# Layer 1's hyperbolic half-steps enter at step 1, their second maxima are dealt over steps 0 to 6, and the formula over steps 6 to 8

## The chip, the cores and the metric

The kernel runs on one core of a Trainium2 chip. The metric is the device time of one execution in microseconds. Durations in the rows below are of one profiled execution.

## The reference

Four sequences (batches) of 1024 tokens with 128 channels pass through two layers. Each layer is attention over 16 heads of 8 channels, then a mixture of experts, both with a layer norm modulated per batch in front. In layer 1 the 16 heads are of three kinds: six ordinary, four hyperbolic, six with normalised queries and keys. The hyperbolic ones are

```
inner = q·k - tq*tk
arg = max(-curv * inner, 1 + 1e-07)
scores = 1 / (1e-06 + sqrt(1/curv) * arccosh(arg)) + causal mask
out = softmax(scores) @ v
```

## The kernel before

**Layout.** The program goes through the batches in turn. Each of its engines has its own written-out program (`tensor_program`, `scalar_program`, `vector_program`, `pool_program`, `sync_program`), and they meet at semaphores. Nothing is scheduled at run time: an engine takes its instructions in the order in which the functions emit them.

**Steps of layer 1's attention.** Heads go in units of four. Units 0, 1 and 2 are ordinary softmax and run one after another, 12 steps each, 36 steps in all. A step is one block of 128 keys against the queries of one half (`c`) of the sequence that may see it; its width is 512, 384, 256 or 128 queries. Widths within a unit are 512, 384, 256, 128, then five times 512, then 384, 256, 128. In step `p` TensorE computes the scores of step p+1 (`scores`), ScalarE takes the exponentials of step p (`std_exp`, L1011, one for each pair of heads), GpSimd cuts the diagonal blocks, and TensorE multiplies with the values (`values`, L747).

**Hyperbolic half-steps.** Unit 3 is hyperbolic. Its 12 steps are split into 24 half-steps of two heads (widths 512, 512, 384, 384, ...), and one half-step enters each ordinary step from `HYP_AT` on. Half-step k passes through: `hyp_scores` (TensorE, L717, last thing in the step in which it enters); one step later `hyp_arg` (VectorE, L1344 and L1349), `hyp_root` (ScalarE, L983 and L984), and a sum on GpSimd (L1624); two steps later `hyp_score` (ScalarE, L989, L992, L995) and `hyp_shift` (VectorE, L1357), which subtracts the row's maximum; three steps later `hyp_exp` (ScalarE, L1000) and `hyp_values` (TensorE, L772).

**Banks.** The scores of ordinary pairs and of hyperbolic half-steps share two pairs of PSUM banks in turn (`take_banks`). So `hyp_scores` in step p waits until ScalarE has taken the first exponential of step p+1, and the second pair of the scores of step p+2 waits for `hyp_arg`'s first instruction.

**Side jobs.** `side_plan` deals further work over the steps: `piece` jobs (TensorE computes a block of scores at L628, with a mask at L631 on the diagonal, and VectorE reduces it to row maxima at L1284), `maxima` jobs on VectorE, `max` jobs that turn the maxima so that they can be sent to DRAM and back, and `turn` jobs for finished outputs. TensorE does up to three side jobs between the scores of a step and the rest after its values. It has two banks for them, so each waits until VectorE has emptied the one before the last. VectorE does about half of a step's side jobs ahead of `hyp_shift` and the rest behind it.

**The maxima of the hyperbolic unit** come in two halves, (0,) for the first 512 rows and (1,) for the rest. Each half passes the same formula as a score: VectorE (L1236, L1242, L1243), ScalarE (L970, L971), VectorE (L1246), ScalarE (L973, L975 four times, L978), VectorE (L1250). Before, `hyp_max` on ScalarE and `maxima` on VectorE run that in one go, at the end of step 4 for half (1,).

Of the kernel before, what the change touches and what calls it, by code (L numbers as in the profile page):

```python
# [86 lines left out]
HYP_AT = 2  # L87
HYP_HALVES = 2 * NS

# [5 lines left out]
POSITIONS = (UNITS * NS, max(3 * NS, HYP_AT + HYP_HALVES + 3) + 1)  # L95
# [7 lines left out]
def score_jobs(l):  # L103

    steps = STD_UNITS[l] * NS
    jobs = [(False, 0, 0), (False, 0, 1)]
    for p in range(POSITIONS[l]):
        if p + 1 < steps:
            jobs += [(False, p + 1, 0), (False, p + 1, 1)]
        if l and 0 <= p - HYP_AT < HYP_HALVES:  # L110
            jobs.append((True, p - HYP_AT, (p - HYP_AT) % 2))
    return jobs
# [5 lines left out]
def output_order(l):  # L118

    outs = [(NS * u + 4 + 8 * c, u, c) for u in range(STD_UNITS[l]) for c in range(NC)]  # L120
    if l:
        outs += [(HYP_AT + 2 * (4 + 8 * c) + 3, HYP_UNIT, c) for c in range(NC)]
    return sorted(outs)
# [5 lines left out]
def side_plan(l, more):  # L129
# [18 lines left out]
    if l == 0:  # L148
        pieces(0, -1, -1)
        plan[-1].append(("max", (0, BOTH)))  # L150
        if more:
            plan[0].append(("out", (0,)))
            plan[1].append(("out", (1,)))
        for u in range(1, UNITS):
            first = NS * (u - 1)
            pieces(u, first, first + NS - 4)
            plan[first + NS - 3].append(("max", (u, BOTH)))
    else:
        pieces(HYP_UNIT, -1, -1, (0,))
        plan[1].append(("max", (HYP_UNIT, (0,))))  # L160
        pieces(HYP_UNIT, 0, 4, (1,))
        plan[6].append(("max", (HYP_UNIT, (1,))))
        pieces(1, 6, 9)
        plan[10].append(("max", (1, BOTH)))
        pieces(2, 13, 21)
        plan[22].append(("max", (2, BOTH)))
        if more:
            for c in range(NC):
                plan[23].append(("xT", (c,)))
                plan[24 + c].append(("stats0", (c,)))  # L170
                plan[26 + c].append(("norm0", (c,)))
                plan[28 + c].append(("hT", (c,)))
                plan[30 + c].append(("kp", (c,)))
        for i, (p, u, c) in enumerate(OUTS[l]):
            plan[min(p + 2, POSITIONS[l])].append(("turn", (i, u, c)))
    n = 0
    for p in sorted(plan):
        items = []
        for kind, what in plan[p]:
            on_pe = kind not in ("maxima", "stats0", "norm0")  # L180
# [58 lines left out]
def adaln_kernel(nc, ins, out):  # L239
    with ExitStack() as ctx:  # L240
# [300 lines left out]
        def tensor_program(pe, b):  # L541
# [18 lines left out]
            def attention(l):  # L560
# [229 lines left out]
                for p in range(POSITIONS[l] + 1):  # L790
# [105 lines left out]
        def scalar_program(act, b):  # L896
# [47 lines left out]
            def attention(l):  # L944
# [21 lines left out]
                def hyp_max(c):  # L966
# [4 lines left out]
                    nc.scalar.activation(z, z, ACT.Exp, scale=0.5).then_inc(hyp_s, 1)  # L971
                    act.wait_ge(hyp_mx, 2 * c + 2)
# [42 lines left out]
                if l:  # L1015
                    hyp_max(0)
                for p in range(POSITIONS[l]):
                    if p < steps:
                        std_exp(p)
                    if l:  # L1020
                        k = p - HYP_AT
                        if 0 <= k - 3 < HYP_HALVES:
                            hyp_exp(k - 3)
                        if 0 <= k - 2 < HYP_HALVES:
                            hyp_score(k - 2)
                        if 0 <= k - 1 < HYP_HALVES:
                            hyp_root(k - 1)
# [61 lines left out]
        def vector_program(dve, b):  # L1089
# [120 lines left out]
            def attention(l):  # L1210
# [6 lines left out]
                def maxima(u, chunks):  # L1217
# [21 lines left out]
                    if is_hyp(l, u):  # L1239

                        c = chunks[0]
# [3 lines left out]
                        dve.wait_ge(hyp_s, 2 * c + 1)  # L1245
                        nc.vector.tensor_tensor(z, z, x, ALU.add).then_inc(hyp_mx, 1)  # L1246
                        dve.wait_ge(hyp_s, 2 * c + 2)
                        if c:
                            dve.wait_ge(a.side, count("max", (HYP_UNIT, (0,))))
                        nc.vector.tensor_scalar(m, z, -1.0, None, ALU.mult).then_inc(a.nmp, 1)  # L1250
# [120 lines left out]
                for p in range(POSITIONS[l] + 1):  # L1371
# [3 lines left out]
                    k = p - HYP_AT  # L1375
                    if l and 0 <= k - 1 < HYP_HALVES:
                        hyp_arg(k - 1)
# [3 lines left out]
                    if l and 0 <= k - 2 < HYP_HALVES:  # L1381
                        hyp_shift(k - 2)
# [162 lines left out]
        def pool_program(pool, b):  # L1545
# [70 lines left out]
            for p in range(POSITIONS[1]):  # L1616
                if p < STD_UNITS[1] * NS:
                    cut(1, p)
                k = p - HYP_AT
                if 0 <= k - 3 < HYP_HALVES:  # L1620
                    hyp_cut(k - 3)
                if 0 <= k - 1 < HYP_HALVES:
                    pool.wait_ge(h_root, k)
                    nc.gpsimd.tensor_tensor(hyp_z(b, k - 1), hyp_z(b, k - 1), hyp_x(k - 1), ALU.add).then_inc(h_sum, 1)  # L1624
# [299 lines left out]
```

## Time and profile before

| | |
|---|---|
| runs without the profiler | 2758.28, 2766.61, 2769.98 us; median 2766.61 |
| the profiled execution | 2764.56 us, span of its instructions 2762.6 us |
| mean granted TensorE clock | 0.81 of full |
| TensorE matmul busy | 2252.7 us (82% of the span) |
| VectorE busy | 1553.4 us (56%) |
| ScalarE busy | 1380.8 us (50%) |
| GpSimd busy | 660.7 us (24%) |

"Busy" is the time in which an engine had an instruction running. A granted clock of 0.5 is 1.2 GHz and 1.0 is 2.4 GHz. The shares are means over very different stages. The change touches only layer 1's attention, which occurs four times, so the rows below come from one of these four.

### The profile page before, as it was taken

Reading aid. Unit: us, or ns where it says so; the run is one execution under the profiler, and the core shown is the slowest. Engines: PE = TensorE matmul, PEld = TensorE weight load, DVE = VectorE, ACT = ScalarE, POOL = GpSimd, SP = SyncE. Lnnn points to the kernel's source line nnn. Section 1 sums busy time; section 2 is a strip of 40 time slices with the busy share of each in tenths; the row PEclk is TensorE's granted clock in tenths of the full one; section 3 lists DMA queues with packets and bytes.
Section 4 is the critical chain, followed back from the end, with each engine's and each line's share of the span. In section 5 each row is a group of like instructions: output and inputs, shape, how many; then the busy total and the mean of one; then the engine's idle time right before and its main releaser. Section 6 shows DMA issues by size and latency. Waiting matters only on the chain. (4 is left out here: it accounts for less than half of the span.)

```text
span 2762.6 us, 30066 instructions
## 1 busy us (share of the span) xinstructions
PE 2252.7 (82%) x10649; PEld 861.1 (31%) x10649; DVE 1553.4 (56%) x3429; ACT 1380.8 (50%) x1963; POOL 660.7 (24%) x639
## 2 busy tenths in 40 slices
PE   3899867778999896777998987768799998677789
PEld 1222432224433242222443234122343324322234
DVE  2564466666555256675655526566655534666542
ACT  1145426894234532898324452489522454268932
POOL 1012202332422210333331120133242111023324
PEclk9599965568999995667999987566799999655689
DMA  5200230001500023100430012210061002300012
GB/s 140 53 19 2 73 81 31 18 1 48 142 23 19 2 77 92 33 2 1 121 89 23 2 37 79 55 33 1 12 151 43 19 1 77 77 31 18 1 43 88
DMA packets 67845, 128.31 MB, mean 46 GB/s; under 512 B 11396, under 2 KB 24836, under 8 KB 63076
## 3 DMA queue, kind: packets, MB, share of 16 engines
q1 hardware_dynamic: 67696, 126.40, 17.2%
q8 instruction: 84, 1.38, 0.2%
q14 instruction: 65, 0.53, 0.1%
HBM read 109.99 MB, written 15.20 MB: 45 GB/s over the span
## 5 line engine op out<-in xcount | busy, mean ns | idle before, releaser
L1284 DVE TENSOR_REDUCE mx<-ps 128x1 f32<-128x512 f32 (+3 forms) x1248 | 641.5, 553 | 461.1 <-PE ps L631 335.9
L1011 ACT ACTIVATE pr<-ps 128x1024 f32<-128x1024 f32 (+3 forms) x672 | 515.9, 804 | 457.6 <-PE ps L701 455.2
L628 PE MATMUL ps<-kop,qop 72*128 72x512 bf16 (+6 forms) x1248 | 455.7, 388 | 142.1 <-DVE mx L1284 103.9
L701 PE MATMUL ps<-qop,kop 75*128 75x512 bf16 (+7 forms) x1344 | 419.6, 379 | 92.3 <-DVE wb L1344 32.7
L1571 POOL TENSOR_SCALAR_AFFINE_SELECT pr<-pr 128x512 f32<-128x512 f32 x224 | 149.5, 668 | 951.6 <-ACT pr L1011 950.6
L747 PE MATMUL ps<-pr,vt 128*32 128x512 f32 (+3 forms) x2688 | 360.4, 615 | 7.2 <-POOL pr L1571 6.1
L1068 ACT ACTIVATE pr<-ps 128x512 f32<-128x512 f32 x224 | 133.8, 597 | 344.1 <-PE ps L854 280.5
L628 PEld LDWEIGHTS ps<-kop,qop 72*128 72x128 bf16 (+1 forms) x1248 | 124.6, 103 | 551.0 <-DVE mx L1284 329.4
L701 PEld LDWEIGHTS ps<-qop,kop 75*128 75x128 bf16 (+1 forms) x1344 | 125.1, 107 | 328.6 <-ACT pr L1011 127.2
L631 PE MATMUL ps<-maskqk,identb 128*128 128x128 bf16 x832 | 202.3, 251 | 0.0
L864 PE MATMUL ps<-pr,w_down 128*128 128x512 f32 x384 | 197.7, 600 | 3.1 <-POOL pr L1562 3.1
L851 PE MATMUL ps<-hT,w_gate 128*128 128x512 f32 x384 | 196.1, 592 | 0.2 <-DVE on L1509 0.2
L754 PE MATMUL ps<-pr,ones 128*32 128x512 f32 (+3 forms) x1536 | 167.3, 508 | 0.0
L1334 DVE COPY osb<-ps 128x512 f32<-128x512 f32 x64 | 44.1, 689 | 213.6 <-PE ps L754 176.0
L1562 POOL TENSOR_TENSOR pr<-on,wb 128x512 f32<-128x512 f32 x84 | 106.3, 1265 | 142.3 <-DVE on L1509 130.9
L854 PE MATMUL ps<-hT,w_up 128*128 128x512 f32 x256 | 130.7, 592 | 0.0
L1344 DVE TENSOR_SCALAR wb<-ps 128x1024 f32<-128x1024 f32 (+3 forms) x96 | 91.7, 955 | 66.2 <-PE ps L717 65.4
L717 PE MATMUL ps<-qop,kop 84*128 84x512 bf16 (+3 forms) x192 | 69.4, 457 | 66.2 <-ACT pr L1011 66.1
L1624 POOL TENSOR_TENSOR wb<-wb 128x1024 f32<-128x1024 f32 (+3 forms) x36 | 72.4, 2010 | 174.1 <-ACT wb L984 174.1
L851 PEld LDWEIGHTS ps<-hT,w_gate 128*128 128x128 f32 x384 | 72.2, 190 | 88.8 <-issue 73.2
L631 PEld LDWEIGHTS ps<-maskqk,identb 128*128 128x128 bf16 x832 | 90.1, 108 | 30.8 <-issue 24.2
L1509 DVE TENSOR_TENSOR on<-pr,ps 128x512 f32<-128x512 f32 x84 | 57.4, 683 | 64.2 <-ACT pr L1068 63.8
(298 smaller groups left out, 3001.8 us busy)
## 6 DMA issues: line engine op xcount, KB each, us to landing
wb<-gates_scratch SPq DMA_DIRECT2D x192, 256.0 KB, 3.3
kop<-kparts_scratch SPq DMA_DIRECT2D x32, 576.0 KB
qop<-qparts_scratch SPq DMA_DIRECT2D x96, 192.0 KB
on<-hmax_scratch SPq DMA_DIRECT2D x8, 1024.0 KB, 5.3
kparts_scratch<-on SPq DMA_DIRECT2D x12, 256.0 KB, 2.9
qparts_scratch<-on SPq DMA_DIRECT2D x12, 256.0 KB, 4.7
qparts_scratch<-wb SPq DMA_DIRECT2D x12, 256.0 KB, 2.9
kparts_scratch<-wb SPq DMA_DIRECT2D x12, 256.0 KB, 2.8
```

Of the source, the lines that this page charges most:

```text
L628: mm = pe.matmul(o, qop[0:k, slot(l, u), j, qb * P:(qb + 1) * P], kop[0:k, slot(l, u), j, k0:k0 + wd], start=True, stop=not diag)
L631: mm = pe.matmul(o[:, wd - P:wd], identb[:], maskqk[:], start=False, stop=True)
L701: mm = pe.matmul(o, kop[0:k, slot(l, u), 2 * pair + j, kb * P:(kb + 1) * P], qop[0:k, slot(l, u), 2 * pair + j, q0:q0 + wd], start=True, s ...
L747: mm = pe.matmul(ps[32 * j:32 * j + 32, 4, o0:o0 + wd], vt[:, kb, 32 * h:32 * h + 32], pr[:, g % 3, j, o0:o0 + wd], start=kb == 0, stop=la ...
L754: mm = pe.matmul(ps[32 * j:32 * j + 32, 5, o0:o0 + wd], ones32[:], pr[:, g % 3, j, o0:o0 + wd], start=kb == 0, stop=last, tile_position=(0 ...
L851: mm = pe.matmul(ps[:, f.gate_banks[i % R], :], wt, h, start=True, stop=True)
L854: mm = pe.matmul(ps[:, 4 + i % 2, :], wt, h, start=True, stop=True)
L864: pe.matmul(ps[:, c, :], wt, fh[:, i % 3, :], start=i < NC, stop=i == f.last[c]).then_inc(g.down, 1)
L1011: nc.scalar.activation(pr[:, g % 3, 2 * pair:2 * pair + 2, o0:o0 + wd], ps[:, bank:bank + 2, o0:o0 + wd], ACT.Exp).then_inc(a.exps, 1)
L1068: nc.scalar.activation(fa[:, i % 3, :], ps[:, f.gate_banks[i % R], :], fn).then_inc(g.act, 1)
L1284: ins_ = nc.vector.tensor_reduce(mx[:, nth(l, u) % 2, j, qb, col % 2:col % 2 + 1], ps[:, bank, 0:wd], AX.X, ALU.max, negate=True)
L1571: nc.gpsimd.affine_select(past, past, [[0, 4], [1, P]], ALU.is_ge, 0.0, base=0, channel_multiplier=-1).then_inc(at[l].cut, 1)
```

## The change

Half-steps enter one ordinary step earlier (`HYP_POS` begins with 1). The 32 pieces of the second maxima are dealt over steps 0 to 6 and no longer over 0 to 4. The `max` job of the first half goes from step 1 to step 0, that of the second half from step 6 to step 9. The formula of the second half is cut in three: VectorE's first part in step 6, its sum in step 7 (`maxima1`), its sign in step 8 (`maxima2`); ScalarE's root stands at the end of step 6 and the rest of its part at the end of step 7. The share of a step's side jobs that VectorE does ahead of `hyp_shift` is rounded down and no longer up. The hyperbolic outputs are copied at steps 12 and 28, before at 13 and 29.

```diff
-HYP_AT = 2
 HYP_HALVES = 2 * NS
+HYP_POS = [1 + k for k in range(HYP_HALVES)]
...
         pieces(HYP_UNIT, -1, -1, (0,))
-        plan[1].append(("max", (HYP_UNIT, (0,))))
-        pieces(HYP_UNIT, 0, 4, (1,))
-        plan[6].append(("max", (HYP_UNIT, (1,))))
+        plan[0].append(("max", (HYP_UNIT, (0,))))
+        pieces(HYP_UNIT, 0, 6, (1,))
         pieces(1, 6, 9)
+        plan[7].append(("maxima1", (HYP_UNIT, (1,))))
+        plan[8].append(("maxima2", (HYP_UNIT, (1,))))
+        plan[9].append(("max", (HYP_UNIT, (1,))))
...
-                        for c in range(NC):
-                            if ("maxima", None, (HYP_UNIT, (c,))) in SIDE[l, more][p]:
-                                hyp_max(c)
+                        if ("maxima", None, (HYP_UNIT, (1,))) in SIDE[l, more][p]:
+                            hyp_max_root(1)
+                        if ("maxima1", None, (HYP_UNIT, (1,))) in SIDE[l, more][p]:
+                            hyp_max(1)
...
+                def hyp_maxima_sum(c):
+
+                    z = of_hyp(nr[:, 0, :], c)
+                    dve.wait_ge(hyp_s, 2 * c + 1)
+                    nc.vector.tensor_tensor(z, z, of_hyp(nr[:, 1, :], c), ALU.add).then_inc(hyp_mx, 1)
...
-                    first = (len(SIDE[l, more][p]) + 1) // 2 if l and k >= 0 else 99
+                    first = len(SIDE[l, more][p]) // 2 if shift != NOBODY else 99
```

On ScalarE, before, from the root of a half-step in step 4 to the first instructions of step 5 (L983 and L984 are `hyp_root`, L970 to L978 the formula of the maxima, L1011 the ordinary exponentials, L1000 `hyp_exp`):

```order
L983 ACTIVATE xn<-xn 128x1024
L984 ACTIVATE xn<-xn 128x1024
L970 ACTIVATE nr<-nr 128x4x4
L971 ACTIVATE nr<-nr 128x4x4
L973 ACTIVATE nr<-nr,consts 128x4x4
L975 ACTIVATE nr<-nr,consts,hyp 128x4 x4
L978 ACTIVATE nr<-nr 128x4x4
L1011 ACTIVATE pr<-ps 128x1024 x2
L1000 ACTIVATE hT<-hT 128x1024
```

And of the change, from the root in step 6 to the end of step 7 (now L995 and L996 are `hyp_root`, L978 and L979 the formula's root, L985 to L990 its rest, L1023 the ordinary exponentials):

```order
L995 ACTIVATE wb<-wb 128x2x256
L996 ACTIVATE wb<-wb 128x2x256
L978 ACTIVATE nr<-nr 128x4x4
L979 ACTIVATE nr<-nr 128x4x4
L1023 ACTIVATE pr<-ps 128x1024 x2
L1012 ACTIVATE wb<-wb 128x2x384
L1001 ACTIVATE hT<-hT,consts 128x2x256
L1004 ACTIVATE hT<-hT,consts,hyp 128x256 x2
L1007 ACTIVATE hT<-hT 128x2x256
L995 ACTIVATE hT<-hT 128x2x256
L996 ACTIVATE hT<-hT 128x2x256
L985 ACTIVATE nr<-nr,consts 128x4x4
```

The formula stood in one piece ahead of step 5's exponentials; now its root stands ahead of step 7's and its long part ahead of step 8's.

On VectorE, before, steps 6 and 7 (L1344 and L1349 are `hyp_arg`, L1292 copies the turned maxima, L1284 reduces a piece, L1357 is `hyp_shift`, L1316 and L1319 are a `turn`):

```order
L1344 TENSOR_SCALAR wb<-ps 128x2x384
L1349 SCALAR_TENSOR_TENSOR wb<-wb 128x2x384
L1292 COPY hrow<-ps 32x128
L1284 TENSOR_REDUCE mx<-ps 128x1 x4
L1357 TENSOR_TENSOR rsb<-rsb,on 128x2x384
L1284 TENSOR_REDUCE mx<-ps 128x1 x4
L1316 RECIPROCAL rec<-ps 128x16
L1319 TENSOR_TENSOR kT<-ps,rec 128x4x8 x4
L1344 TENSOR_SCALAR wb<-ps 128x2x256
L1349 SCALAR_TENSOR_TENSOR wb<-wb 128x2x256
L1284 TENSOR_REDUCE mx<-ps 128x1 x3
L1357 TENSOR_TENSOR wb<-wb,on 128x2x384
```

And of the change, the end of step 6 and step 7 (L1376 and L1381 are `hyp_arg`, L1316 reduces a piece, L1389 is `hyp_shift`, L1348 and L1351 the `turn`, L1273 the formula's sum):

```order
L1389 TENSOR_TENSOR wb<-wb,on 128x2x384
L1316 TENSOR_REDUCE mx<-ps 128x1 x6
L1348 RECIPROCAL rec<-ps 128x16
L1351 TENSOR_TENSOR kT<-ps,rec 128x4x8 x4
L1376 TENSOR_SCALAR wb<-ps 128x2x256
L1381 SCALAR_TENSOR_TENSOR hT<-wb 128x2x256
L1316 TENSOR_REDUCE mx<-ps 128x1 x3
L1389 TENSOR_TENSOR wb<-wb,on 128x2x256
L1316 TENSOR_REDUCE mx<-ps 128x1 x3
L1273 TENSOR_TENSOR nr<-nr 128x4x4
```

The sum of the formula is now VectorE's last instruction of step 7, behind six pieces and the shift.

## Rows read from the trace of the kernel before

**Rows 1.** The page, part 1: busy time, share and instructions of each engine.

```profile
PE 2252.7 (82%) x10649; PEld 861.1 (31%) x10649; DVE 1553.4 (56%) x3429; ACT 1380.8 (50%) x1963; POOL 660.7 (24%) x639
```

**Rows 2.** Busy time by stretch: length, then PE, PEld, DVE, ACT, POOL; PEclk; DMA.

```profile
428.00:446.00 18.00, 16.22 (x60) 4.03 (x57) 15.39 (x22) 10.14 (x12) 2.98 (x2) 0.51 0.03 11
...
413.76:451.36 37.60, 29.11 (x113) 8.09 (x113) 25.55 (x44) 17.25 (x27) 7.23 (x6) 0.55 0.08 30
...
1080.10:1118.34 38.24, 30.24 (x113) 8.36 (x113) 25.69 (x44) 17.26 (x28) 7.24 (x6) 0.54 0.08 28
...
451.36:459.41 8.05, 6.45 (x18) 0.97 (x18) 3.52 (x4) 7.95 (x10) 0.41 (x1) 0.52 0.00 1
...
503.15:627.87 124.72, 96.38 (x391) 29.78 (x391) 83.85 (x155) 111.79 (x148) 45.69 (x36) 0.60 0.04 10
...
413.76:645.11 231.35, 180.58 (x784) 54.96 (x784) 149.11 (x279) 184.76 (x253) 69.62 (x63) 0.64 0.05 15
```

**Rows 3.** Timeline of ScalarE: the exponentials of steps 4, 5, 8, 11, 13, 20, 29.

```profile
437.65 1.92 ACT L1011 ACTIVATE pr<-ps 128x1024 f32<-128x1024 f32 x2
...
451.36 1.92 ACT L1011 ACTIVATE pr<-ps 128x1024 f32<-128x1024 f32 x2
...
476.13 1.92 ACT L1011 ACTIVATE pr<-ps 128x1024 f32<-128x1024 f32 x2
...
497.02 0.64 ACT L1011 ACTIVATE pr<-ps 128x256 f32<-128x256 f32 x2
...
511.44 1.49 ACT L1011 ACTIVATE pr<-ps 128x768 f32<-128x768 f32 x2
...
577.62 1.92 ACT L1011 ACTIVATE pr<-ps 128x1024 f32<-128x1024 f32 x2
...
629.98 1.94 ACT L1011 ACTIVATE pr<-ps 128x1024 f32<-128x1024 f32 x2
```

**Rows 4.** Timeline, end of step 4.

```profile
446.85 1.29 DVE L1284 TENSOR_REDUCE mx<-ps 128x1 f32<-128x512 f32 x2 [0.69 <-PE ps L631]
...
448.93 0.22 ACT L970 ACTIVATE nr<-nr 128x16 f32<-128x16 f32 x1 [2.90 <-DVE nr L1243]
...
452.42 0.82 PE L717 MATMUL ps<-qop,kop 84*128 84x384 bf16 x2 [5.07 <-ACT pr L1011]
```

**Rows 5.** Timeline, the first half-step, from TensorE's start of step 2.

```profile
427.43 0.28 PE L701 MATMUL ps<-qop,kop 72*128 72x128 bf16 x2
...
431.98 1.06 PE L717 MATMUL ps<-qop,kop 84*128 84x512 bf16 x2
...
435.60 1.06 ACT L983 ACTIVATE hT<-hT 128x1024 f32<-128x1024 f32 x1 [6.62 <-DVE hT L1349]
...
437.83 2.35 POOL L1624 TENSOR_TENSOR hT<-hT,wb 128x1024 f32<-128x1024 f32 x1 [8.14 <-ACT hT L984]
...
440.21 1.15 ACT L989 ACTIVATE hT<-hT,consts 128x1024 f32<-128x1024 f32 x1 [0.64 <-POOL hT L1624]
...
442.94 1.06 ACT L995 ACTIVATE hT<-hT 128x1024 f32<-128x1024 f32 x1
```

**Rows 6.** Timeline: TensorE's starts of steps 6 to 10, VectorE's last pieces of step 7.

```profile
461.38 0.60 PE L701 MATMUL ps<-qop,kop 72*128 72x512 bf16 x2 [0.41 <-ACT pr L1011]
...
472.98 1.06 PE L701 MATMUL ps<-qop,kop 72*128 72x512 bf16 x2
...
479.45 1.67 DVE L1284 TENSOR_REDUCE mx<-ps 128x1 f32<-128x128 f32 x3 [2.30 <-PE ps L631]
...
480.25 0.49 PE L701 MATMUL ps<-qop,kop 72*128 72x384 bf16 x2
...
487.91 0.38 PE L701 MATMUL ps<-qop,kop 72*128 72x256 bf16 x2
...
493.48 0.28 PE L701 MATMUL ps<-qop,kop 72*128 72x128 bf16 x2
```

**Rows 7.** Timeline of ScalarE: the hyperbolic exponential of step 17.

```profile
553.04 1.06 ACT L1000 ACTIVATE rsb<-rsb 128x1024 f32<-128x1024 f32 x1 [2.06 <-DVE rsb L1357]
```

More of the change, by code:

```diff
@@ L94 @@
 STD_UNITS = (UNITS, UNITS - 1)
-POSITIONS = (UNITS * NS, max(3 * NS, HYP_AT + HYP_HALVES + 3) + 1)
+POSITIONS = (UNITS * NS, max(3 * NS, HYP_POS[-1] + 4) + 1)
 def nth(l, u):
@@ L109, in score_jobs @@
             jobs += [(False, p + 1, 0), (False, p + 1, 1)]
-        if l and 0 <= p - HYP_AT < HYP_HALVES:
-            jobs.append((True, p - HYP_AT, (p - HYP_AT) % 2))
+        if l and hyp_at(p) != NOBODY:
+            jobs.append((True, hyp_at(p), hyp_at(p) % 2))
     return jobs
@@ L121, in output_order @@
     if l:
-        outs += [(HYP_AT + 2 * (4 + 8 * c) + 3, HYP_UNIT, c) for c in range(NC)]
+        outs += [(HYP_POS[2 * (4 + 8 * c) - 1] + 4, HYP_UNIT, c) for c in range(NC)]
     return sorted(outs)
@@ L179, in side_plan @@
         for kind, what in plan[p]:
-            on_pe = kind not in ("maxima", "stats0", "norm0")
+            on_pe = kind not in ("maxima", "maxima1", "maxima2", "stats0", "norm0")
             items.append((kind, n if on_pe else None, what))
@@ L795, in attention @@
                         values(p, extra)
-                    if l and 0 <= p - HYP_AT - 3 < HYP_HALVES:
-                        hyp_values(p - HYP_AT - 3)
+                    if l and hyp_at(p - 3) != NOBODY:
+                        hyp_values(hyp_at(p - 3))
                     for x in extra:
                         side_job(*x)
-                    if l and 0 <= p - HYP_AT < HYP_HALVES:
-                        hyp_scores(p - HYP_AT)
+                    if l and hyp_at(p) != NOBODY:
+                        hyp_scores(hyp_at(p))
                 if l:
@@ L1244, in maxima @@
                                                        op1=ALU.mult).then_inc(hyp_mx, 1)
[L1245 to L1250, printed above, removed]
+                        if chunks[0] == 0:
+                            hyp_maxima_sum(0)
+                            hyp_maxima_sign(0)
                         return
@@ L1259, in side_job @@
                         maxima(*what)
+                        return
+                    if kind == "maxima1":
+                        hyp_maxima_sum(1)
+                        return
+                    if kind == "maxima2":
+                        hyp_maxima_sign(1)
                         return
@@ L1374, in attention @@
                             outputs_out(i)
-                    k = p - HYP_AT
-                    if l and 0 <= k - 1 < HYP_HALVES:
-                        hyp_arg(k - 1)
-                    first = (len(SIDE[l, more][p]) + 1) // 2 if l and k >= 0 else 99
+                    shift = hyp_at(p - 2) if l else NOBODY
+                    if l and hyp_at(p - 1) != NOBODY:
+                        hyp_arg(hyp_at(p - 1))
+                    first = len(SIDE[l, more][p]) // 2 if shift != NOBODY else 99
                     for x in SIDE[l, more][p][:first]:
                         side_job(*x)
-                    if l and 0 <= k - 2 < HYP_HALVES:
-                        hyp_shift(k - 2)
+                    if shift != NOBODY:
+                        hyp_shift(shift)
                     for x in SIDE[l, more][p][first:]:
```

42 lines of the change are left out of this document (27 added, 15 removed).

## The prediction

> **What bounds the kernel now.** The page says only that TensorE is busy for 82% of the span [rows 1]. The change touches one stage that occurs four times, so I went to that stage. I took as milestones the starts of ScalarE's ordinary exponentials, written E4 for step 4's, E5 and so on [rows 3], and asked for the busy times between them [rows 2]. The first of the four attentions runs from E0 at 413.76 to its last exponential at 645.11: 231.35 us, of which ScalarE is busy 184.76 and TensorE 180.58. The reader should see two regimes. From E12 to E28 (503.15 to 627.87) ScalarE works 111.79 of 124.72 us and is the bound. In steps 0 to 4 it works 17.25 of 37.60 us, and TensorE, with 29.11 us, sets the pace together with its waits on VectorE. The second batch shows the same (17.26 of 38.24). So ScalarE has 20 us of room early in each attention.
>
> Then the end of step 4 [rows 4]. VectorE reduces the last piece until 448.14; ScalarE has waited 2.90 us when it gets its first formula instruction at 448.93, and only behind the formula comes E5, at 451.36. TensorE, whose next half-step scores need E5, stands for 5.07 us. That is the visible bubble.
>
> **The change part by part**, in batch 0's times; times four at the end. I follow the milestones and give each after-time by its chain.
>
> *Steps 0 to 4.* Through step 1 the side jobs are 11 pieces and no longer 15, with 1,280 fewer columns. At about 0.5 us a piece (VectorE takes 1.29 us for two of 512 [rows 4], less for narrow ones) TensorE gains 2.1 us, so it begins the first half-step's scores at 427.43 - 2.1 = 425.3, where it now begins step 2 [rows 5]. From that start to the root takes 3.6 us (431.98 to 435.60), so the root starts at 428.9. Root 2.1 (two of 1.06), GpSimd 2.35 and a hand-over, score 3.8 (440.21 to 444.00) [rows 5] bring 437.3; the second root, 2.1, stands between this and E4. E4 comes at 439.4, before 437.65. But then step 4's ScalarE work is lighter: exponentials 1.9, one `hyp_exp` 1.06, score 3.7, root of width 384 1.7, less 0.1 where they overlap, and no formula. **E5 at 447.7, 3.7 us earlier**, with one half-step more in flight. The bubble of 5.07 goes; 1.7 of it is given back by the latency of the first half-step, which no ordinary work is long enough to cover.
>
> *Steps 4 to 7, the pieces.* What TensorE no longer does in steps 0 to 4 it does in 5 and 6: four and three pieces more, 3,584 columns. Before, the last reduction of step 4 ended 10.5 us after E4 [rows 3, 4]. It now has 0.5 us less of pieces and 1.9 us of `hyp_values` more: TensorE begins step 5 at about 450.8. Step 5 took 8.05 us with TensorE busy 6.45 [rows 2]; four masked pieces of 0.66 fill the idle part and lengthen it to 9.3: step 6 at 460.1. Step 6 took 11.6 (461.38 to 472.98) [rows 6]; three pieces of 0.75, less the `max` job, make it 13.6: step 7 at 473.7.
>
> *The formula in step 7.* This is the price that I hold against the change. `maxima1` is VectorE's last instruction of step 7, and ScalarE's `hyp_max` waits for it in front of E8. Before, E8 was at 476.13 while VectorE ended step 7's pieces at 481.12 [rows 3, 6]: ScalarE was 5 us ahead there, and this order takes the lead away. Queued behind the waiting instruction are E8, then TensorE's half-step scores (banks), then VectorE's `hyp_arg`. VectorE ends 8.1 us after TensorE's start of step 7; the sum is 0.2; the rest of the formula 1.9 (E5 minus 448.93 is 2.43 for all of it, less the root). **E8 at 483.9, 7.8 us later than before.** At step 6 the same wait costs little: `maxima` stands in the first half of VectorE's side jobs, about 1.5 us behind ScalarE's root, and this is inside step 6's TensorE-bound time.
>
> *Steps 8 to 12.* TensorE begins step 8 1.3 us behind E8, at 485.2. Step 8 took 7.66 us and loses 0.4 (a narrower half-step); step 9 took 5.57 and gains 0.3 (`max`) and 0.8 (half-step 8 is 512 wide and now comes here) [rows 6]. Step 10 starts at 499.1, `hyp_arg` 2.5 and root 2.1 follow: E11 at 503.8 against 497.02, +6.8. Steps 11 and 12 become ScalarE-bound: 6.9 + 8.8 against 14.4 before [rows 3], so E13 is +8.1. The broadcast of the second maxima is issued two steps before its first use, about 15 us, and costs nothing; were that cover gone, VectorE would stand at step 11's shift.
>
> *Steps 13 to 19.* Half-steps are all 512 wide in either order, so nothing moves but the share of side jobs ahead of the shift. In step 16 it goes from four of seven to three: the fourth is the first that TensorE sends behind its values, and the shift had waited for it. ScalarE's 2.06 us in step 17 [rows 7] go, and 0.3 in step 14: -2.4, E20 at +5.7.
>
> *Steps 20 to 28.* The narrow half-steps come one step earlier and the last step is empty. What was moved forward is missing here: ScalarE has 0.4 us less in step 20, 0.65 less in each of 21 to 25, 1.0 in 26 and in 27, 0.1 in 28, in all 5.7. From E20 (577.62) to E29 (629.98) [rows 3] it is nearly always the bound, so I take it whole: **E29 at 0.0.** Behind it nothing changes.
>
> The sum per attention is -3.7 + 11.5 - 1.0 + 1.3 - 2.4 - 5.7 = 0.0, and four times that is 0 on the profiled execution's 2764.56 us. That execution lies 2 us under the median of the runs; I say **2766 us**. The head start is real and the bubble of step 4 goes, but the formula's new place opens another of nearly its size at step 7.
>
> *A rule against the trace.* In steps 2 to 4 TensorE is busy 16.22 of 18.00 us and has a granted clock of 0.51, which is 1.2 GHz [rows 2]. The Trainium skill ("TensorE: Matmul & The Clock Gate", part 1) says that the default state is throttled and activity releases the throttle. By that rule these steps would run at 2.4 GHz; the trace disagrees, so my sum takes piece prices at 1.2 GHz.
>
> **The rivals.**
>
> *Slower: the end does not give it back.* The 5.7 us of steps 20 to 28 need ScalarE to be the bound there. Between E12 and E28 it has 12.9 us without work [rows 2], so some of these steps end on TensorE or VectorE. If none of it is won, the time is 4 x 5.7 = 23 us longer, 2789. It decides against "no change" once more than 3.5 us of the 5.7 fail, or the wait in front of E8 is that much longer. Chance 0.28.
>
> *Faster: TensorE is not late in steps 5 and 6.* If the added pieces fit into waits, step 7 starts at 470 and no longer at 473.7, and everything behind it moves up by 3.7 us: 4 x 3.7 = 15, 2751. For it speaks that in step 5 TensorE idles 1.6 us of 8.05 [rows 2]; against it that pieces wait for VectorE too. If the release rule above applied to the busier steps, it would end here as well: at 2.4 GHz the seven moved pieces of about 0.7 us halve, 2.4 us per attention, and with the matmuls of steps 4 to 6 the 3.7 is reached. I give the clock 0.05 of this case. Chance in all 0.32.
>
> *The formula doesn't get in the way.* If ScalarE found `maxima1` done when it arrives, E8 would be at about 478.4 and the time 4 x 5.5 = 22 us shorter, 2744. The order of rows speaks against it, since VectorE has a shift and three pieces between ScalarE's score and that sum. It is in the 0.32.
>
> **How the numbers follow.** Forecast, near 2766, 0.40 (its own range 2753 to 2779); faster 0.32; slower 0.28. Half a percent, 14 us, is about what a measurement of this kernel can tell from no change, and is the border of the three. The unknown sizes are the two lengths of steps 5 and 6 (each ±1.5 us), step 2's latency (±1) and the end (0 to 5.7). The range takes both rivals in: 2743 to 2790.
>
> **What would show it.** E5 about 4 us earlier relative to E0, with no 5 us wait of TensorE at the end of step 4. In step 7, ScalarE's first instruction of the formula's rest (now L985) with some 5 us of idle ahead of it, released by VectorE's sum L1273, and TensorE's half-step scores of step 7 waiting 3 us for ScalarE. E8 7 to 8 us later, E13 8 later. The 2.06 us wait of step 17 gone. Wrong would be: L985 without a wait (then faster), E20 to E29 as long as before (then slower), or VectorE waiting for the maxima's DMA in front of step 11's shift.

## The result and the profile after

The changed kernel takes 2746.46 us (median of five runs, 2741.61 to 2749.26) against 2766.61 us for the kernel before: ratio 0.9923, interval 0.9900 to 0.9947, 20 us less. The forecast was no change, 2766 us. The time lies in the stated range of 2743 to 2790 us, but outside the forecast's own part of it (2753 to 2779) and past its border of 14 us: it is in the case "faster", which had a chance of 0.32. The profiled execution of after took 2746.46 us, with a span of 2743.8 us and a mean granted clock of 0.828. Page part 1 of after, which answers to [rows 1]:

```profile
PE 2207.1 (80%) x10649; PEld 854.9 (31%) x10649; DVE 1544.6 (56%) x3429; ACT 1377.5 (50%) x1963; POOL 653.3 (24%) x639
```

The same 10,649 matmuls now keep TensorE busy for 45.6 us less. The other engines lose 3 to 9 us.

Below, E0, E5 and so on are again the starts of ScalarE's ordinary exponentials of a step. This table gives them in us after E0, as means over the four attentions, read from the timeline of ScalarE; E35 is the start of the last one. It includes seven of the experiments, which are told further down.

| | E4 | E5 | E7 | E8 | E11 | E13 | E17 | E18 | E20 | E24 | E26 | E29 | E35 |
|---|---|---|---|---|---|---|---|---|---|---|---|---|---|
| before | 24.0 | 37.7 | 53.2 | 62.4 | 82.2 | 96.7 | 133.6 | 144.0 | 161.7 | 192.7 | 204.6 | 213.5 | 229.4 |
| after | 24.3 | 32.3 | 46.9 | 62.3 | 82.5 | 99.2 | 137.2 | 145.6 | 162.7 | 189.5 | 202.2 | 209.2 | 224.5 |
| early_only | 27.7 | 41.7 | 55.9 | 65.0 | 87.4 | 104.2 | 142.5 | 152.8 | 170.6 | 197.5 | 208.1 | 215.1 | 231.3 |
| enter_at_2 | 19.7 | 28.0 | 43.9 | 60.4 | 78.4 | 93.5 | 130.4 | 139.0 | 156.5 | 186.0 | 199.6 | 208.6 | 225.2 |
| pieces_0_4 | 27.8 | 39.8 | 55.7 | 64.1 | 85.7 | 102.5 | 140.3 | 148.8 | 165.8 | 192.2 | 205.5 | 212.5 | 228.3 |
| round_up | 23.7 | 31.7 | 46.3 | 61.5 | 83.4 | 100.2 | 138.4 | 148.7 | 166.5 | 193.4 | 204.0 | 211.0 | 227.2 |
| before_round_down | 22.2 | 35.9 | 51.4 | 60.7 | 81.4 | 95.9 | 133.7 | 142.4 | 159.6 | 189.6 | 203.1 | 212.1 | 229.0 |
| sum_first_in_7 | 23.7 | 31.8 | 47.2 | 57.6 | 77.7 | 94.5 | 132.9 | 141.5 | 159.3 | 186.6 | 199.6 | 207.0 | 223.7 |
| sum_first_round_23 | 25.1 | 33.2 | 47.7 | 58.5 | 77.0 | 93.7 | 132.1 | 140.7 | 158.5 | 185.3 | 196.3 | 203.4 | 218.7 |

An attention is 4.9 us shorter (229.4 - 224.5), four are 19.5 us, and that is the whole gain of this profile: what is left of the span outside E0 to E35 is 1845 us before and 1846 us after. The mean hides a wide spread. From E0 to E35 the four attentions take 230.7, 227.7, 229.0 and 230.1 us before and 224.9, 228.6, 225.9 and 218.6 us after, so over half of the gain stands in the last one, which in both kernels has no side jobs for a next batch, and the second gains nothing.

The windows of steps 4, 5, 6 and 7 in the first attention of after follow (E4 is at 439.97, E8 at 477.86), then E0 to E5, E12 to E28 and the whole attention. Up to E5 ScalarE now works 20.98 of 31.91 us, where it had 17.25 of 37.60. The columns are those of [rows 2].

```profile
439.97:448.02 8.05, 6.90 (x24) 1.82 (x24) 5.65 (x8) 7.95 (x10) 2.76 (x2) 0.50 0.01 2
448.02:455.43 7.41, 6.04 (x24) 1.68 (x24) 5.87 (x9) 7.31 (x10) 2.21 (x2) 0.73 0.00 0
455.43:462.56 7.13, 6.15 (x34) 1.63 (x30) 4.69 (x11) 7.00 (x13) 2.39 (x3) 0.91 0.00 1
462.56:477.86 15.30, 10.11 (x42) 3.46 (x42) 10.49 (x24) 8.02 (x17) 3.21 (x3) 0.75 0.00 0
416.11:448.02 31.91, 24.32 (x105) 6.99 (x105) 21.56 (x34) 20.98 (x26) 7.60 (x7) 0.61 0.12 39
505.11:622.12 117.01, 80.78 (x376) 25.57 (x377) 80.57 (x149) 105.71 (x142) 41.55 (x35) 0.73 0.03 8
416.11:641.64 225.53, 161.78 (x784) 51.65 (x784) 147.86 (x279) 183.89 (x253) 68.12 (x63) 0.73 0.06 16
```

In steps 4, 5 and 6 ScalarE has 0.1 us without work in each: 7.95 of 8.05, 7.31 of 7.41, 7.00 of 7.13. It sets these three steps, whose pieces on TensorE and VectorE lie beside its work. Step 7 is different: 15.30 us, of which ScalarE works 8.02. Of the rest, 2.68 us stand ahead of its root, which waits for VectorE's `hyp_arg` (L1381; the same wait was 1.40 us before), and 4.43 us ahead of the formula. The timeline in after, where the number in brackets is the idle time ahead and what ended it:

```profile
468.46 1.06 PE L709 MATMUL ps<-qop,kop 72*128 72x512 bf16 x2
...
474.51 1.51 DVE L1316 TENSOR_REDUCE mx<-ps 128x1 f32<-128x128 f32 x3 [2.13 <-PE ps L639]
475.93 0.17 DVE L1273 TENSOR_TENSOR nr<-nr 128x16 f32<-128x16 f32 x1
476.13 0.31 ACT L985 ACTIVATE nr<-nr,consts 128x16 f32<-128x16 f32 x1 [4.43 <-DVE nr L1273]
477.86 1.92 ACT L1023 ACTIVATE pr<-ps 128x1024 f32<-128x1024 f32 x2
478.92 0.39 PE L725 MATMUL ps<-qop,kop 84*128 84x128 bf16 x2 [3.67 <-ACT pr L1023]
```

The chain reads from the top. VectorE's last three pieces of the step, its sum (L1273), ScalarE's formula (L985), which waited 4.43 us, the exponentials of step 8, and TensorE's half-step scores, which waited 3.67 us for them. This is the bubble that the prediction described. It comes from a better position, though: E8 is where it was before (62.3 against 62.4), not 7.8 us later.

Three smaller waits are new or longer. ScalarE has 2.83 us of idle ahead of a root in step 10 (1.36 before), and in steps 24 and 25 it waits for VectorE's statistics of the next layer norm (L961):

```profile
494.78 1.06 ACT L995 ACTIVATE wb<-wb 128x1024 f32<-128x1024 f32 x1 [2.83 <-DVE wb L1381]
...
611.18 0.30 ACT L961 ACTIVATE sd<-mv,consts 128x4 f32<-128x4 f32 x1 [1.27 <-DVE mv L1300]
...
617.15 0.30 ACT L961 ACTIVATE sd<-mv,consts 128x4 f32<-128x4 f32 x1 [1.01 <-DVE mv L1300]
```

Those statistics are side jobs that stood in VectorE's first half of the step. With the half rounded down they stand behind the shift.

### The profile page after: what moved, and what is told of

It reads as the page before. It is cut to its first block and busy times, and to the rows that moved or that the text cites. A ratio compares the mean times of both kernels' runs of the same rounds, so it can differ in the third digit from the quotient of the medians.

```text
span 2743.8 us, 30066 instructions
## 1 busy us (share of the span) xinstructions
PE 2207.1 (80%) x10649; PEld 854.9 (31%) x10649; DVE 1544.6 (56%) x3429; ACT 1377.5 (50%) x1963; POOL 653.3 (24%) x639
## 5 line engine op out<-in xcount | busy, mean ns | idle before, releaser
L1316 DVE TENSOR_REDUCE mx<-ps 128x1 f32<-128x512 f32 (+3 forms) x1248 | 639.8, 553 | 431.8 <-PE ps L639 326.7
L1023 ACT ACTIVATE pr<-ps 128x1024 f32<-128x1024 f32 (+3 forms) x672 | 515.5, 804 | 434.3 <-PE ps L709 431.9
L636 PE MATMUL ps<-kop,qop 72*128 72x512 bf16 (+6 forms) x1248 | 444.1, 378 | 146.8 <-DVE mx L1316 110.3
L709 PE MATMUL ps<-qop,kop 75*128 75x512 bf16 (+7 forms) x1344 | 408.2, 369 | 110.8 <-DVE wb L1376 43.6
L755 PE MATMUL ps<-pr,vt 128*32 128x512 f32 (+3 forms) x2688 | 350.2, 599 | 6.3 <-POOL pr L1603 5.6
L1376 DVE TENSOR_SCALAR wb<-ps 128x1024 f32<-128x1024 f32 (+3 forms) x96 | 91.5, 953 | 66.4 <-PE ps L725 65.0
L1541 DVE TENSOR_TENSOR on<-pr,ps 128x512 f32<-128x512 f32 x84 | 57.4, 683 | 62.4 <-ACT pr L1082 62.0
```

The source lines that it names most:

```text
L636: mm = pe.matmul(o, qop[0:k, slot(l, u), j, qb * P:(qb + 1) * P], kop[0:k, slot(l, u), j, k0:k0 + wd], start=True, stop=not diag)
L709: mm = pe.matmul(o, kop[0:k, slot(l, u), 2 * pair + j, kb * P:(kb + 1) * P], qop[0:k, slot(l, u), 2 * pair + j, q0:q0 + wd], start=True, s ...
L755: mm = pe.matmul(ps[32 * j:32 * j + 32, 4, o0:o0 + wd], vt[:, kb, 32 * h:32 * h + 32], pr[:, g % 3, j, o0:o0 + wd], start=kb == 0, stop=la ...
L1023: nc.scalar.activation(pr[:, g % 3, 2 * pair:2 * pair + 2, o0:o0 + wd], ps[:, bank:bank + 2, o0:o0 + wd], ACT.Exp).then_inc(a.exps, 1)
L1316: ins_ = nc.vector.tensor_reduce(mx[:, nth(l, u) % 2, j, qb, col % 2:col % 2 + 1], ps[:, bank, 0:wd], AX.X, ALU.max, negate=True)
```

## The experiments

Ratios are to the kernel before, on the same chip, with a 95% interval; medians of before were 2766.7, 2766.4 and 2764.7 us in the three groups (22 to 27 runs each). The chapter goes by question.

### Is TensorE the bound of steps 5 and 6?

**double_pieces** computes each of the seven pieces of steps 5 and 6 twice, into the same bank. Nothing is left out.

```diff
+    late = is_hyp(l, u) and any(w_ == what for s in (5, 6) for _, _, w_ in SIDE[l, more][s])
+    for _ in range(2 if late else 1):
         mm = pe.matmul(o, qop[...], kop[...], start=True, stop=not diag)
```

> The changed kernel in which TensorE computes each of the seven second-maxima pieces of steps 5 and 6 twice, with its mask; nothing else is added. Theory P (the prediction's: TensorE sets the length of steps 5 and 6): E6 and E7 move back by about 1.2 us in each of the two steps, E8 to 65 us after E0, the total 8 to 12 us longer, 2755 to 2759. Rival A (ScalarE sets steps 5 and 6, which took 7.4 and 7.2 us with ScalarE busy all the time): E7 stays at 47 us; only the end of step 7 on TensorE may move, by less than 1.5 us: 2744 to 2751.

Measured: 2749.87 us (12 runs), 0.9946 (0.9929 to 0.9963), as the rival of the expectation has it. The windows of its steps 5 and 6 in the first attention (E5 is at 446.42, E7 at 460.96):

```profile
446.42:453.83 7.41, 6.33 (x29) 1.58 (x28) 5.86 (x9) 7.31 (x10) 2.21 (x2) 0.92 0.00 0
453.83:460.96 7.13, 6.00 (x42) 2.36 (x40) 5.26 (x13) 7.00 (x13) 2.86 (x3) 1.00 0.00 1
```

TensorE has 5 matmuls more in the first (four pieces and one mask) and 8 in the second (three pieces and three masks are 6, the other two lie across the window's borders or are missing records of after), and the steps last 7.41 and 7.13 us, to the hundredth what after has. Over the attentions, E7 is at 47.3 (after 46.9) and E8 at 62.3 (62.3). So the pieces of steps 5 and 6 are covered by ScalarE's work, even in double number. TensorE's busy time hardly moved, from 6.04 to 6.33 and from 6.15 to 6.00 us, since the granted clock rose too, from 0.73 to 0.92 and from 0.91 to 1.00. What double pieces would cost at 1.2 GHz, no run shows.

### What is each part of the change worth?

**early_only** takes the kernel before and makes the half-steps enter one step earlier, with the first half's `max` job moved along. **enter_at_2** is the changed kernel with the half-steps entering where they did.

```diff
 early_only, against before:
-HYP_AT = 2
+HYP_AT = 1
-        plan[1].append(("max", (HYP_UNIT, (0,))))
+        plan[0].append(("max", (HYP_UNIT, (0,))))
 enter_at_2, against after:
-HYP_POS = [1 + k for k in range(HYP_HALVES)]
+HYP_POS = [2 + k for k in range(HYP_HALVES)]
```

> The kernel before with one part of the change: half-steps enter at step 1 and the max job of the first half goes to step 0. Pieces stay in steps 0 to 4, the formula in one go at step 4, rounding up. Theory A (early entry alone moves a half-step's ScalarE work from the end into idle time): E20 to E29 falls from 51.8 to 46 to 47 us in the mean, the early part loses 1 to 3 us since steps 0 to 4 now hold all pieces and a half-step more: 2750 to 2758. Rival B (without the dealing the early steps give all of it back): 2762 to 2770.

> The changed kernel with the half-steps entering at step 2 again; dealing, formula in three parts and rounding stay. Theory A (the gain is ScalarE work moved from the end, steps 20 to 28, into ScalarE's idle time of steps 0 to 4): the stretch E20 to E29, which fell from 51.8 us (mean of the four attentions) to 46.5, goes back to about 52, E5 comes no earlier than 32 us after E0, and most of the 20 us is lost: 2760 to 2768. Rival B (the gain is the spread work and the formula off step 4, the entry is nothing): the time stays at 2744 to 2750.

Measured: early_only 2776.84 us (12 runs), 1.0037 (1.0019 to 1.0055); enter_at_2 2750.89 us (10 runs), 0.9945 (0.9924 to 0.9966). The first is worse than both of its theories, the second just past the upper end of its rival's range. Alone, the early entry loses 10 us. The bubble at the end of step 4 stays as it was in [rows 4], as two rows of early_only's timeline show:

```profile
450.29 0.22 ACT L970 ACTIVATE nr<-nr 128x16 f32<-128x16 f32 x1 [3.34 <-DVE nr L1243]
...
453.78 0.82 PE L717 MATMUL ps<-qop,kop 84*128 84x384 bf16 x2 [5.20 <-ACT pr L1011]
```

E4 and E5 come 3.7 and 4.0 us later, because the first half-step now goes through steps that are full of pieces. From E5 to E20 it loses another 4.9 us (128.9 against 124.0). The shorter end (E20 to E29 is 44.5 us against 51.8) brings back 7.3 us, and E35 is at 231.3. In the changed kernel the early entry costs 4.3 us up to E5 (28.0 in enter_at_2, 32.3 in after) and brings 5.7 at the end (E20 to E29: 52.1 and 46.4). Between E5 and E20 it costs 2.0 more. At E35 it is worth 0.7 us per attention, and 0.0022 of the time by the two ratios, less than their intervals can tell apart.

**pieces_0_4** is the changed kernel with the pieces dealt over steps 0 to 4 as before, and the formula, still in three, over steps 4 to 6.

```diff
-        pieces(HYP_UNIT, 0, 6, (1,))
+        pieces(HYP_UNIT, 0, 4, (1,))
-        plan[7].append(("maxima1", (HYP_UNIT, (1,))))
-        plan[8].append(("maxima2", (HYP_UNIT, (1,))))
+        plan[5].append(("maxima1", (HYP_UNIT, (1,))))
+        plan[6].append(("maxima2", (HYP_UNIT, (1,))))
```

> The changed kernel with the pieces dealt over steps 0 to 4 again, the formula in steps 4, 5 and 6. Theory A (TensorE sets steps 2 to 4, so fewer pieces there bring E5 forward; and the sum is cheap in a step without pieces): E5 2 to 3 us later than 31.9 after E0, steps 5 and 6 not longer than 7.5, no wait of 4 us in front of the formula's rest; E8 at 60 to 63, the total 2742 to 2752. Rival B (dealing over 0 to 6 carries the gain): 2756 to 2764. Rival C (the wait at step 7 was the main loss and goes with it): below 2738.

Measured: 2759.35 us (12 runs), 0.9980 (0.9957 to 1.0002), in the range of the expectation's rival B. E5 is 7.4 us later than in after (39.8, 32.3); E8, without the wait of step 7, gets all but 1.8 us of it back (64.1, 62.3), and E35 is 3.9 us later. Dealing the pieces to step 6, with the formula behind them, is worth 0.0057, about 16 us. It is the largest part that is seen in the attention itself.

**round_up** is the changed kernel with the share of side jobs ahead of the shift rounded up again. **before_round_down** is the kernel before with that share rounded down.

```diff
 round_up, against after:
-                    first = len(SIDE[l, more][p]) // 2 if shift != NOBODY else 99
+                    first = (len(SIDE[l, more][p]) + 1) // 2 if shift != NOBODY else 99
 before_round_down, against before:
-                    first = (len(SIDE[l, more][p]) + 1) // 2 if l and k >= 0 else 99
+                    first = len(SIDE[l, more][p]) // 2 if l and 0 <= k - 2 < HYP_HALVES else 99
```

> The changed kernel with the share of side jobs ahead of the shift rounded up again. Theory A: ScalarE's wait for the shift in step 17, 2.06 us before, comes back and a little in step 14, E13 to E20 from 63.5 us back to 65.1: 2752 to 2756. Rival B (those waits only move into VectorE's and TensorE's slack): 2744 to 2749.

> The kernel before with only the rounding of the share of side jobs ahead of the shift changed (down). Theory A: ScalarE's 2.06 us in step 17 go, E13 to E20 from 65.1 to 63.5 us: 2758 to 2762. Rival B: no change, 2765 to 2768.

Measured: round_up 2769.47 us (12 runs), 1.0021 (0.9999 to 1.0044); before_round_down 2766.16 us (12 runs), 1.0004 (0.9984 to 1.0024). The first is longer than either of its theories had it, the second is as its rival B. Without the rounding the whole gain is gone; in the kernel before, it brings nothing. The profile explains a part of this. In round_up ScalarE waits in step 15 and in step 17, there as in [rows 7]:

```profile
541.22 1.06 ACT L1012 ACTIVATE xn<-xn 128x1024 f32<-128x1024 f32 x1 [3.66 <-DVE xn L1389]
...
560.02 1.06 ACT L1012 ACTIVATE wb<-wb 128x1024 f32<-128x1024 f32 x1 [1.72 <-DVE wb L1389]
```

The second of them is at 553.30 in after and has no wait. E17 to E18 takes 10.3 us in round_up and 8.5 in after. The wait of step 15 stands neither in after nor in before. The earlier copy of the first hyperbolic outputs has moved its `turn` job from step 15 to step 14, which now has seven side jobs and no longer six, so that rounding up puts a fourth piece ahead of the shift. early_only, which rounds up as well, has this wait too (3.65 us). It is one reason why the rounding matters more in the changed order, though steps 14 and 15 together are only 0.3 us longer in round_up (21.4 and 21.1), since after waits elsewhere in them. From E13 to E20 round_up takes 66.3 us, after 63.5, before 65.1. Against that, the statistics behind the shift cost after 2.1 us (E24 to E26 takes 12.7 and 10.6). E35 is 2.8 us later in round_up, 11 us for four. The other 10 us or so of its span lie outside the attentions, where the change does nothing (1856 us in this profile, 1846 in after's). That part stays open. In the kernel before, rounding down shortens E17 to E18 as well (10.5 to 8.7), and E24 to E26 gets longer by 1.7 (11.8 to 13.6). At E29 1.4 us are left, at E35 0.4: in between stand the same instructions in both, and that stretch took 16.9 us and not 15.8. The last section comes back to it.

**before_down_to_22** is the kernel before, rounded down up to step 22 and up from step 23, so that the statistics stay ahead of the shift.

```diff
+                    first = (len(SIDE[l, more][p]) + (p >= 23)) // 2 if l and 0 <= k - 2 < HYP_HALVES else 99
```

> The kernel before with the share of side jobs ahead of the shift rounded down in steps 4 to 22 and up from step 23. Theory A (rounding down wins 2 us in steps 16 and 17 and gives 1.5 us back in steps 24 and 25, where the layer-norm statistics now stand behind the shift and ScalarE waits for them): E24 to E26 back from 13.5 to 12.0 us, 4 to 8 us less than rounding down everywhere: 2758 to 2763. Rival B (the two are unrelated, the longer end comes from TensorE's clock): 2764 to 2768, E24 to E26 stays at 13.5.

Measured: 2764.15 us (12 runs), 1.0002 (0.9988 to 1.0016), the time of rival B with the step lengths of theory A. E24 to E26 is 11.8 us again, as it should be. The milestones run 2.0 us ahead of before at E20 (159.7) and 1.9 at E29 (211.6). At E35 (229.3) nothing is left of it, again in the stretch with the same instructions. So the wait of the statistics is real, but its removal doesn't show in the time of the kernel before.

**formula_one_go** is the changed kernel with the second half's formula in one piece, at the end of step 6. VectorE does its first part and its sum in step 6, ScalarE its root and its rest at the end of that step; the `max` job stays at step 9.

```diff
+                        hyp_maxima_sum(chunks[0])
+                        hyp_maxima_sign(chunks[0])
...
-        plan[7].append(("maxima1", (HYP_UNIT, (1,))))
-        plan[8].append(("maxima2", (HYP_UNIT, (1,))))
```

> The changed kernel with the second maxima's formula in one go in step 6 (VectorE, ScalarE, VectorE, as before at step 4); the max job stays at step 9. Theory A (the split puts a wait of 4.4 us in front of E8, because ScalarE waits for VectorE's last instruction of step 7): that wait goes, step 6 gets 2 us longer since the maxima stand in the first half of VectorE's side jobs and are done when ScalarE arrives, TensorE's stall of 3.67 us in step 7 goes; E8 about 59 us after E0 against 62.3, 2 to 3 us gained per attention, 2735 to 2742. Rival B (the split in three is where the change gains): 2755 to 2762.

Measured: 2738.80 us (6 runs), 0.9910 (0.9883 to 0.9937), against 0.9923 for after. E7 comes 3.1 us later (50.1), since the formula is a single chain in front of it, and E8 3.0 us earlier (59.3), since step 7 has no wait for the formula. Cutting the formula in three brings nothing that these runs can see.

### What does the wait of step 7 cost?

**act_behind_exp8** moves ScalarE's rest of the formula behind the exponentials of step 8. **sum_first_in_7** moves VectorE's sum to the front of step 7's side jobs.

```diff
 act_behind_exp8:
                     if p < steps:
                         std_exp(p)
+                    if l and p and ("maxima1", None, (HYP_UNIT, (1,))) in SIDE[l, more][p - 1]:
+                        hyp_max(1)
...
-                        if ("maxima1", None, (HYP_UNIT, (1,))) in SIDE[l, more][p]:
-                            hyp_max(1)
 sum_first_in_7:
-        plan[7].append(("maxima1", (HYP_UNIT, (1,))))
+        plan[7].insert(0, ("maxima1", (HYP_UNIT, (1,))))
```

> The changed kernel with ScalarE's part of the formula that stood at the end of step 7 placed behind the two ordinary exponentials of step 8. Theory A (the wait in front of E8, 4.43 us, and TensorE's stall of 3.67 us behind it are a loss of the change's own): E8 at 57 to 58 us after E0 against 62.3, of which 2.5 to 3.5 us per attention reach the end: 2732 to 2738. Rival B (TensorE and VectorE are the bound in steps 7 to 10, so ScalarE only waits elsewhere, in front of the roots of steps 8 to 10): 2743 to 2748.

> The changed kernel with VectorE's sum of the formula first among step 7's side jobs and no longer last. Theory A: ScalarE finds it done, only the 1.75 us of the formula's rest stand in front of E8: E8 at 58 to 59 us after E0, 2 to 3 us per attention at the end: 2734 to 2740. Rival B as for the placement behind step 8's exponentials: 2743 to 2748.

Measured: act_behind_exp8 2746.58 us (6 runs), 0.9909 (0.9882 to 0.9936); sum_first_in_7 2734.94 us (6 runs), 0.9876 (0.9850 to 0.9903). Both take the wait out of E8's way: 56.2 and 57.6, where after has 62.3. In act_behind_exp8 the formula then stands in step 8, which lasts 9.7 us (after 5.5; L985 still waits 2.44 us there), and E35 is at 225.3. Its median equals after's, as rival B had it, and its interval doesn't tell the two apart. In sum_first_in_7 nothing takes the place of the wait; its timeline has these two rows of ScalarE:

```profile
467.72 0.29 ACT L985 ACTIVATE nr<-nr,consts 128x16 f32<-128x16 f32 x1
...
469.43 1.92 ACT L1023 ACTIVATE pr<-ps 128x1024 f32<-128x1024 f32 x2
```

L985 runs with no idle time ahead of it, and E8 follows 1.7 us later. The lead of 4.7 us at E8 shrinks from E17 on (4.2 at E18, 3.5 at E20, 2.2 at E29), and 0.7 is left at E35 in this profile (its E29 to E35 takes 16.8 us, after's 15.3). By the medians it is some 12 us faster, as theory A had it, but four times 0.7 is 3 us, so the profile doesn't show that these 12 us come from the wait. The intervals of this kernel and after overlap a little (0.9903, 0.9900), so its gain over after is likely and not certain.

### The two combined

**sum_first_round_23** puts the sum first and rounds up from step 23 on. **one_go_max_8** is formula_one_go with the `max` job at step 8 and the same rounding.

```diff
 both:
-                    first = len(SIDE[l, more][p]) // 2 if shift != NOBODY else 99
+                    first = (len(SIDE[l, more][p]) + (p >= 23)) // 2 if shift != NOBODY else 99
 one_go_max_8 alone:
-        plan[9].append(("max", (HYP_UNIT, (1,))))
+        plan[8].append(("max", (HYP_UNIT, (1,))))
```

> The changed kernel with VectorE's sum of the formula first in step 7 and the share of side jobs rounded up from step 23 on. Theory A: both gains add, E24 to E26 from 13.0 to about 11 us without ScalarE's waits of 1.27 and 1.01 us for the statistics: 5 to 8 us under the version with the sum first alone (2735): 2727 to 2731. Rival B (the end behind step 26 takes it back): 2733 to 2737.

> The changed kernel with the formula in one go in step 6, the max job of the second half in step 8 and no longer 9, and the rounding up from step 23. Theory A: against the version in one go alone (2739) the end gains 5 to 8 us by the rounding; the max job a step earlier takes 0.3 us of VectorE's work out of step 9, in front of the first wide root, and gains up to 1 us per attention: 2728 to 2734. Rival B: no change by either, 2737 to 2741.

Measured: sum_first_round_23 2730.67 us (6 runs), 0.9884 (0.9863 to 0.9904), the lowest median of all; one_go_max_8 2744.26 us (6 runs), 0.9927 (0.9901 to 0.9953). Three rows of ScalarE in the first:

```profile
466.89 0.29 ACT L985 ACTIVATE nr<-nr,consts 128x16 f32<-128x16 f32 x1
...
602.35 0.28 ACT L961 ACTIVATE sd<-mv,consts 128x4 f32<-128x4 f32 x1
...
607.21 0.28 ACT L961 ACTIVATE sd<-mv,consts 128x4 f32<-128x4 f32 x1
```

The waits of after at these three instructions are gone, E24 to E26 takes 11.0 us (sum_first_in_7 13.0), and E35 is at 218.7. It can't be told from sum_first_in_7 by the ratios, and its interval, which ends at 0.9904, is clear of 1 and overlaps after's (from 0.9900) by little. So it beats the kernel before, and very likely after. Its time is in the range of its theory A; one_go_max_8's is above both of its theories. one_go_max_8's attention was short in the profile (E35 220.9, span 2728.6 us), but its median was some 13 us above that execution. With the earlier `max` job and the rounding no gain over formula_one_go shows.

## Where the forecast was right and where it was wrong

The stated range held only because it took in the faster rival; the forecast itself, no change, did not come true. The terms per attention, as the prediction put them and as the means over four attentions show them:

| stretch | predicted | measured |
|---|---|---|
| E0 to E5 | -3.7 | -5.4 |
| E5 to E8 | +11.5 | +5.3 |
| E8 to E11 | -1.0 | +0.3 |
| E11 to E13 | +1.3 | +2.4 |
| E13 to E20 | -2.4 | -1.6 |
| E20 to E29 | -5.7 | -5.3 |
| E29 to E35 | 0 | -0.5 |
| sum | 0.0 | -4.9 |

**The step that failed is the one headed "Steps 4 to 7, the pieces".** It added the moved pieces to TensorE's time as if TensorE set steps 5 and 6: step 6 at 460.1 and step 7 at 473.7, that is 46.3 and 59.9 us after E0. TensorE began them at these rows of after, 41.3 and 52.4 us after its E0 of 416.11 (the second is the first row of step 7's timeline above):

```profile
457.41 0.60 PE L709 MATMUL ps<-qop,kop 72*128 72x512 bf16 x2
```

As means over the four attentions TensorE began step 5 at 34.3 us, where the sum had 37.0, took 7.4 us for it (predicted 9.3) and 11.4 us for step 6 (predicted 13.6). So 4.1 of the 6.8 us come from the two steps, and 2.7 from what lies ahead of them: E4 came 1.4 us earlier than in the sum, and the end of step 4 was 1.3 us shorter. ScalarE sets steps 5 and 6 in after. [rows 2] had shown it already: in step 5 of before ScalarE is busy 7.95 of 8.05 us and TensorE 6.45. I read the 1.6 us of TensorE's idle time, put 2.6 us of pieces in it and let the rest lengthen the step. It wasn't a wait for something that the pieces would push back, and double_pieces shows that even twice their number doesn't. The pieces were also priced too high: of the four of step 5 only one has a mask, where the sum took four masked ones of 0.66 us. Its additions are off by a little besides (439.4 + 10.5 - 0.5 + 1.9 is 451.3 and not 450.8, and 8.05 - 1.6 + 2.6 is 9.1 and not 9.3), which nearly cancels. The rival "TensorE is not late in steps 5 and 6" came true, at 2751 against 2746. That the two numbers are so close is in part luck: it put 3.7 us on the start of step 7, which came 6.8 us early, and the stretches from E8 to E20 took 3.2 us of that back.

**The wait of step 7 was right in cause and size.** L985 waited 4.43 us (predicted some 5) for L1273, TensorE's half-step scores 3.67 (predicted 3), and two experiments that take the wait away from E8 bring it to 56.2 and 57.6. What was off was only the time at which it began. The rival without this wait (2744) has a number close to the result, but its mechanism did not occur.

**Steps 0 to 4** gained 1.7 us more than predicted. E4 was to come 1.75 us later and came 0.3 later. The first half-step's scores start 10.2 us after E0 in the first attention (426.30), where I had 11.5. The prediction's side remark on latency was right in sign: the early entry costs 4.3 us up to E5 when all else is in place. It is mostly the dealing of the pieces, and not the entry, that removes the bubble at the end of step 4: E4 to E5 takes 13.7 us in before, 14.0 in early_only, 12.0 in pieces_0_4, where the formula is in three, 8.3 in enter_at_2 and 8.1 in after.

**Steps 8 to 12** were 2.4 us worse than the two terms said (+2.7 for both, predicted +0.3). Steps 11 and 12 became ScalarE-bound as predicted, but there ScalarE also has the 2.83 us ahead of the root in step 10. What causes that wait wasn't tried by itself.

**Rounding.** The 2.4 us of steps 13 to 19 came out at 1.6, with the wait of step 17 gone; the 0.3 us of step 14 didn't come, since its wait is 2.58 us in both kernels. The working didn't see that other jobs move with the same rule: the statistics of steps 24 and 25, 2.5 to 3.5 us in each of the three attentions that have them and nothing in the fourth (E24 to E26 takes 14.3, 13.3, 13.3 and 9.9 us in after, 10.8, 10.8, 10.8 and 9.9 in round_up). It said that nothing else moves in steps 13 to 19, but a `turn` job went from step 15 to step 14. Nor did it see that the rounding pays only in the changed order (round_up against before_round_down). More than half of the 27 us that the ratios give it (0.0098) isn't found in the attention (11 us), and stays open.

**Steps 20 to 28** were right, 5.3 for 5.7: ScalarE is the bound there. In after it works 42.5 of 48.0 us from E20 to E29 of the first attention, before 48.9 of 52.4. The slower rival rested on this and fell.

**The clock.** TensorE's mean granted clock over the first attention rose from 0.64 [rows 2] to 0.73, and its busy time for 784 matmuls fell from 180.58 to 161.78 us; as means over the four the clock went from 0.65 to 0.71. The prediction gave a faster clock 0.05 of its case. In steps 5 and 6 the clock was 0.73 and 0.91, so the moved pieces were cheaper than at 1.2 GHz. But since ScalarE is the bound there, the length of these steps hardly hangs on it: in the second attention of after step 6 had a clock of 0.63 and took 7.45 us, not 7.13, and TensorE began step 7 1.3 us later than in the first. What the faster clock gives the rest of the attention, where TensorE is busy most of some stretches, no run separates from the new order. The Trainium skill ("TensorE: Matmul & The Clock Gate", part 1) says that activity releases the throttle. The rise in double_pieces agrees with it (0.73 to 0.92 in step 5, 0.91 to 1.00 in step 6); steps 2 to 4 of before, 16.22 of 18.00 us busy at 0.51, don't.

## What to carry to other kernels

Work that is moved into a step is priced by what bounds that step: read every engine's busy time in the step's own window, and where another engine is at 7.3 of 7.4 us, the moved work may cost nothing, as here even its double did. A cross-engine wait placed at the end of a step stands in front of the next step's first instruction, and other engines queue up behind it (4.43 us on ScalarE, then 3.67 on TensorE). One line that put the awaited instruction first brought the next step forward by 4.7 us; how much of that reaches the end is a question of its own (0.7 us in the profile). And a rule such as "half, rounded down" moves every job that falls under it: list them all before it is priced, in both orders.

## What was unexpected of the hardware

A stretch with the same instructions takes different times within one execution. These windows of before run from the start of step 29 to just behind that of step 35, in the first three attentions:

```profile
629.98:645.11 15.13, 14.59 (x102) 5.19 (x100) 5.11 (x15) 11.23 (x15) 2.31 (x4) 1.00 0.00 1
1290.60:1308.50 17.90, 17.36 (x106) 6.22 (x104) 5.11 (x15) 11.34 (x15) 2.31 (x4) 0.87 0.01 1
1955.70:1973.80 18.10, 17.56 (x106) 6.47 (x105) 5.11 (x15) 11.47 (x15) 2.31 (x4) 0.85 0.00 1
```

[rows 2] gave only the first attention's mean clock. With TensorE busy 96 to 97% of the time in all three, the granted clock is 1.00, 0.87 and 0.85, and the stretch takes 15.13, 17.90 and 18.10 us. (The first window holds 4 matmul records fewer.) Why the clock differs, nothing here shows. The kernel before ran between 2751 and 2781 us in 27 runs. A single profiled execution therefore can't carry a difference of 10 us between two kernels, and where the runs and the profile differ by that much (round_up, sum_first_in_7, one_go_max_8) I leave it open. The same holds for the tables above: each kernel's milestones are of one execution, so a difference of a microsecond or two at E35 may be chance. At E5 the two kernels are clear of each other: 36.8 to 38.2 us in the attentions of before, 31.8 to 33.6 in those of after.
